# Two mixtures of experts around an attention: the second product of each block turned round, so that it gives rows at once

## Time and profile before

| | us |
|---|---|
| median of 3 runs | 1285.2 (1285.19 to 1287.82) |
| the profiled execution | 1283.73 |
| its span in the profile | 1282.0 |
| TensorE busy | 1144.8 (89%) |
| VectorE busy | 1124.8 (88%) |
| ScalarE busy | 878.0 (68%) |
| GpSimd busy | 518.6 (40%) |

### The profile page before, as it was taken

How to read it: one execution, slowest core, us unless ns; L and a number is a source line. 1 busy time by engine, 2 the same in 40 slices (tenths; PEclk the granted TensorE clock), 3 DMA queues, 4 the chain that set the end, 5 groups by cost and what they waited for, 6 DMA issues and landing times.

```text
span 1282.0 us, 27027 instructions
## 1 busy us (share of the span) xinstructions
PE 1144.8 (89%) x9003; PEld 606.4 (47%) x9003; DVE 1124.8 (88%) x2287; ACT 878.0 (68%) x1849; POOL 518.6 (40%) x672
## 2 busy tenths in 40 slices
PE   3857999888699999999999999999999999999993
PEld 2745888877322222332223223222222367788882
DVE  7877888887799999989999999999999778988885
ACT  1223555555289999898889888898887965455651
POOL 3883556424224001525336333445344128543232
PEclk9999999999689999999999999999999999999997
DMA  8115565563110200012011000010000413555653
GB/s 278 53 63 181 206 204 194 196 238 137 51 51 18 68 18 4 16 31 55 2 31 37 21 18 18 20 42 10 18 9 25 147 72 142 193 206 191 243 200 141
DMA packets 58746, 123.28 MB, mean 96 GB/s; under 512 B 12736, under 2 KB 33954, under 8 KB 58576
## 3 DMA queue, kind: packets, MB, share of 16 engines
q1 hardware_dynamic: 49616, 103.57, 23.6%
q0 software_dynamic: 8704, 16.93, 4.2%
q10 hardware_dynamic: 288, 1.05, 0.2%
HBM read 36.39 MB, written 23.62 MB: 47 GB/s over the span
## 4 chain that ended last, share of the span: by engine, by line
PE 59%; DVE 25%; POOL 6%; issue 5%; DMA 3%; ACT 2%; SPq 1%; DVEq 0%; POOLq 0%; ACTq 0%
PE psum L2329 15%; DVE att_neg_part L1996 13%; PE psum L2301 9%; PE psum L2232 8%; PE psum L2220 7%; PE psum L2222 7%; PE psum L2283 6%; POOL rows_dram L1293 4%; DVE ffn_x2c L1938 2%; DMA ffn_block_rows<-rows_dram 2%; DVE ffn_hidden L1949 2%; DVE stats L1631 1%; PE psum L2307 1%; ACT ffn_silu L1454 1%; PE psum L2172 1%
## 5 line engine op out<-in xcount | busy, mean ns | idle before, releaser
L1996 DVE TENSOR_REDUCE att_neg_part<-psum 128x2 f32<-128x1024 f32 x512 | 594.7, 1215 | 27.0 <-PE psum L2283 24.9
L1486 ACT ACTIVATE att_probs<-psum 128x512 f32<-128x512 f32 x1024 | 556.4, 597 | 59.8 <-PE psum L2301 23.0
L2329 PE MATMUL psum<-att_probs,att_values 128*18 128x256 f32 x4096 | 322.2, 387 | 4.3 <-issue 3.7
L2283 PE MATMUL psum<-att_right,att_left 62*128 62x512 f16 x1024 | 288.1, 391 | 31.0 <-DVE att_neg_part L1996 30.1
L1454 ACT ACTIVATE ffn_silu<-ffn_x2c,ffn_rec 128x256 f32<-128x256 f32 (+1 forms) x320 | 154.7, 487 | 170.4 <-DVE ffn_x2c L1938 169.9
L1309 POOL DMA_INDIRECT y_dram<-ffn_y,ffn_block_rows x144 | 142.6, 990 | 233.9 <-ACT ffn_y L1472 205.5
L2301 PE MATMUL psum<-att_right,att_left 64*128 64x512 f16 x512 | 199.0, 389 | 0.1
L2307 PE MATMUL psum<-att_right,att_left 64*128 64x512 f16 x512 | 194.9, 381 | 0.0
L1938 DVE TENSOR_SCALAR ffn_x2c<-psum,ffn_rec 128x256 f32<-128x256 f32 (+1 forms) x320 | 162.6, 512 | 34.0 <-PE psum L2222 29.7
L2220 PE MATMUL psum<-ffn_block_t,ffn_rec 128*128 128x256 f32 (+1 forms) x640 | 178.7, 361 | 1.8 <-ACT ffn_block_t L1405 1.8
L2222 PE MATMUL psum<-ffn_block_t,ffn_rec 128*128 128x256 f32 (+1 forms) x640 | 178.0, 360 | 0.0
(11 more groups left out here) (236 smaller groups left out, 1040.8 us busy)
## 6 DMA issues: line engine op xcount, KB each, us to landing
ffn_rec<-record SPq DMA_DIRECT2D x80, 776.5 KB, 3.8
ffn_block_rows<-rows_dram SPq DMA_DIRECT2D x64, 130.0 KB, 3.1
record<-in_L_ffn_W SPq DMA_DIRECT2D x16, 256.0 KB, 6.4
att_left<-q_parts_dram SPq DMA_DIRECT2D x64, 64.0 KB, 2.2
att_right<-att_max_parts SPq DMA_DIRECT2D x256, 1.0 KB
y_dram<-ffn_y,ffn_block_rows POOLq DMA_INDIRECT x144, 2.3
x_sb<-in_L_attn_x SPq DMA_DIRECT2D x4, 512.0 KB, 7.1
record<-in_L_ffn_Wo SPq DMA_DIRECT2D x8, 256.0 KB, 7.2
```

The costliest lines, as they stand in the source:

```text
L1486: S.activation(probs[:, slot % PROBS, :], ring_bank(("score", slot))[:, :], ACT.Exp, scale=unlift).then_inc(att_bank.by_act, 1)
L1996: V.tensor_reduce(out=neg_part[:, h % 2, keys, p::PAIR, t], in_=psum[:, low:high + 1, :], axis=AX.X, op=ALU.max, negate=True).then_inc(red ...
L2283: product = TE.matmul(bank[max_banks(n)[k]], left[s][PRODUCTS[k], p, q], right[s][PRODUCTS[k], p, seen], start=True, stop=True)
L2329: last = TE.matmul(value_bank[g * VS:g * VS + 2 * VW, p * HALF // 2:(p + 1) * HALF // 2], values_flat[:, at:at + 2 * VW], queries, start=( ...
```

## The change

- `tensor_second`: hidden is loaded and Wo is streamed, in pieces of 128 rows: 8 matmuls of 128 columns for a long block where there were 4 of 256. y comes out with its rows on the partitions. `y_bank` has that shape; `back_bank`, `tensor_turn_back`, the buffer `y_t` and the semaphore `y_turned_back` are gone.
- bo lies along the free axis now. It leaves the record; instead SP loads it as a broadcast row for every block (`bo_rows`, 128 x 128 numbers, one more DMA in `sync_load_record`), and VectorE adds it out of PSUM (`vector_add_y`, in the place of `vector_clip_y`). That add now waits for the scatter of three blocks ago, and frees the seat (`y_added` in place of `biased`).
- The clip of y goes to GpSimd (`pool_clip_y`), behind the scatters of the block before; `scalar_weigh` waits for it and works in place in SBUF. `scalar_bias` is gone.
- Attention's first matmul waits for `y_added` where it waited for `weighed`.

```diff
         def sync_next_block(k, i):
-            Q.wait_ge(biased, k * BLOCKS + i - SLOTS[k] + 1)
+            Q.wait_ge(y_added, k * BLOCKS + i - SLOTS[k] + 1)
             sync_load_record(k, i)
...
             Q.dma_start(mix[k].rec[:, seat(k, i), :].unsqueeze(1),
                         record[:, bass.ds(expert, 1), :]).then_inc(mix[k].rec_in[seat(k, i)], 16)
+            Q.dma_start(mix[k].bo_rows[:, seat(k, i), :],
+                        bo[bass.ds(expert, 1), :].to_broadcast([P, F])).then_inc(mix[k].rec_in[seat(k, i)], 16)
...
                 if at >= 2:
                     pool_scatter_results(k, at - 2)
+                if 1 <= at <= BLOCKS:
+                    pool_clip_y(k, at - 1)
+
+        def pool_clip_y(k, i):
+            n = k * BLOCKS + i
+            G.wait_ge(y_added, n + 1)
+            y = mix[k].y[:, n % YSETS, 0:tiles_of(n), :]
+            G.tensor_scalar(y, y, LIMIT, -LIMIT, ALU.min, ALU.max).then_inc(y_clipped, 1)
...
-        def scalar_bias(k, i):
...
         def scalar_weigh(k, i):
             n, s = k * BLOCKS + i, seat(k, i)
-            S.wait_ge(turned_back, n + 1)
-            if n >= YSETS:
-                S.wait_ge(scattered_y[n % YSETS], y_scatters(n, n % YSETS))
+            S.wait_ge(y_clipped, n + 1)
             for r in range(tiles_of(n)):
-                last = S.activation(mix[k].y[:, n % YSETS, r, :], back_bank[n % 2][:, r * P:(r + 1) * P], ACT.Copy,
+                last = S.activation(mix[k].y[:, n % YSETS, r, :], mix[k].y[:, n % YSETS, r, :], ACT.Copy,
                                     scale=mix[k].block_rows[:, i % ROW_SLOTS, r, GATE:GATE + 1])
...
-        def vector_clip_y(k, i):
...
+        def vector_add_y(k, i):
+            n, s = k * BLOCKS + i, seat(k, i)
+            tiles = tiles_of(n)
+            V.wait_ge(product, n + 1)
+            if n >= YSETS:
+                V.wait_ge(scattered_y[n % YSETS], y_scatters(n, n % YSETS))
+            V.tensor_tensor(mix[k].y[:, n % YSETS, 0:tiles, :], y_bank[n % 2][:, 0:tiles, :],
+                            mix[k].bo_rows[:, s, :].unsqueeze(1).to_broadcast([P, tiles, F]), ALU.add).then_inc(y_added, 1)
...
         def tensor_attention():
-            TE.wait_ge(weighed, BLOCKS)
+            TE.wait_ge(y_added, BLOCKS)
...
             TE.wait_ge(hidden_ready, n + 1)
             if n >= 2:
-                TE.wait_ge(biased, n - 1)
-            few = slice(0, rows_of(n))
-            for c in range(HC):
-                last = TE.matmul(y_bank[n % 2][:, few], mix[k].rec[:, s, WO + c * F:WO + (c + 1) * F], mix[k].hidden[:, n % 2, c, few],
-                                 start=(c == 0), stop=(c == HC - 1))
+                TE.wait_ge(y_added, n - 1)
+            for r in range(tiles_of(n)):
+                for c in range(HC):
+                    last = TE.matmul(y_bank[n % 2][:, r, :], mix[k].hidden[:, n % 2, c, r * P:(r + 1) * P],
+                                     mix[k].rec[:, s, WO + c * F:WO + (c + 1) * F], start=(c == 0), stop=(c == HC - 1))
             last.then_inc(product, 1)
```

More of the change, by code:

```diff
@@ L413, in build_macaron @@
         product = semaphore("second_product")
-        biased = semaphore("y_biased")
+        y_added = semaphore("y_added")
         y_clipped = semaphore("y_clipped")
-        turned_back = semaphore("y_turned_back")
         weighed = semaphore("y_weighed")
@@ L1594, in vector_fold @@
             V.wait_ge(fold_dve, 2)
-            V.tensor_copy(record[:, :, BO], bo_col)
             V.tensor_scalar(record[:, :, CLIP_LO:CLIP_LO + HC], bias[1], -1.0, -X2_LIMIT,
@@ L1894, in build_macaron @@
         chunk_bank = [bank[0], bank[1], bank[2], wide[0][:, 0:512]]
-        y_bank = [bank[3][:, 0:BLOCK], wide[1][:, 0:BLOCK]]
+        y_bank = [rows[:, 0:BH * F].rearrange("p (r f) -> p r f", r=BH) for rows in (bank[3], wide[1])]
         turn_bank = [bank[5][:, 0:BLOCK], bank[5][:, BLOCK:2 * BLOCK]]
-        back_bank = [bank[3][:, BLOCK:2 * BLOCK], wide[1][:, BLOCK:2 * BLOCK]]
         def vector_experts(k):
```

49 lines of the change are left out of this document (9 added, 40 removed).

## The result

The changed kernel takes 1298.8 us (median of 4 runs, 1296.8 to 1301.9) against 1285.8 (4 runs, 1285.2 to 1287.8): ratio 1.0098, 95% interval 1.0085 to 1.0110. It is slower, by 13 us in the medians; the two profiled executions, spans 1296.1 and 1282.0, differ by 14.1.

What follows compares the result with a forecast made beforehand. TensorE was taken to pace long blocks, VectorE close behind, rows' transfers the first mixture's short blocks. Terms -7.5 + 1.5 + 5 + 7.5 + 4 - 1.7 = +8.8 gave 1292.5, put on the median: 1294 us (1280 to 1306).

Steps and rivals of the forecast that it cites:

- the sum: All terms against the profiled execution's 1283.73 us: -7.5 + 1.5 + 5 + 7.5 + 4 - 1.7 = +8.8.
- One of its own signs of being wrong: Long blocks: the prediction counts as wrong if the pitch between chores isn't 5.45 us.
- TensorE's pace, -7.5: Long blocks: turns back save 0.22, second product 1.78 against 1.73; net -0.17 in 44 blocks, 7.5 us gained.
- the VectorE-bound blocks' +1.5: VectorE's add replacing its clip costs 0.1 in 15 blocks where VectorE is the bound: 1.5 us.
- The rule for which weight loads would not hide: Second product: loads overlap only across differing row groups, giving product near 3.4, block near 7.1; rival 1340, chance 0.01.
- GpSimd's queue in the first mixture, +5: Blocks 16 to 19 and 21: clip behind chores makes ScalarE's weighing 8.1 late; holes recover 3, cost 5 (2.5 to 10).
- the lower bound 0.35: GpSimd's clip of y: lowest price, from half a 512-column cast at 0.605; 1.1 taken, range 0.35 to 1.5.
- GpSimd's queue in the second mixture, +7.5: Block 2's clip waits behind chores and scatters, weighing 7.6 later; with later blocks 7.5 us (5 to 10).
- SP and the short blocks, +4: First mixture's short blocks: rows asked for 0.45 later plus new DMA's 0.50; 4 x 1.0 = 4 us (2.5 to 6).
- Into attention, -1.7: Last second product to attention's first matmul: 2.3 us becomes the add's 0.5, saving 1.7.
- the clip and VectorE fight over the port: SBUF port in every block: 0.5 to 0.9 each over 64 long blocks, up to 40 us, 1310 and more; chance 0.07.

Runs made afterwards that it cites:

- the second set: Second of three sets of four kernels: kernel before, changed kernel, bo transfer behind the rows, both costs away; the kernel before took 1285.1 us there.
- e4: Kernel before, with only the second product in 8 matmuls of 128 columns instead of 4 of 256, weights and moving operand unchanged; 1.0079 of the kernel before.
- r2: Changed kernel, unmodified, run again in the second set; 1.0115 of the kernel before.
- e7: Changed kernel with bo loaded only once into each seat and GpSimd's clip of y left out; 0.9975 of the kernel before.
- r3: Changed kernel without GpSimd's clip of y, repeated in the third set; 1.0081 of the kernel before.
- r4: Changed kernel with bo loaded only once into each seat, GpSimd's clip kept, repeated in the third set; 1.0000 of the kernel before.
- e5: Changed kernel with the bo transfer issued after the rows' transfer of the same block instead of ahead of it; 1.0067 of the kernel before.
- e8: Kernel before plus an unread transfer of a quarter of the expert's bo to 128 partitions behind each record; 1.0041 of the kernel before.
- e1: Changed kernel without GpSimd's clip of y, in the first set; 1.0084 of the kernel before.

## Why the prediction was right

It said 1294 us (1280 to 1306), slower with 0.63; it is 1298.8, so the loss is 13.0 where the sum had 8.8. The mechanism was right in the two parts that carry the loss, the queue in the second mixture and the short blocks; of the sizes, two were well off. One of its own signs of being wrong came about: the pitch is 5.54, not 5.45. By its terms, measured in the second set:

- **TensorE's pace, -7.5.** The turns back are gone as forecast, but the second product takes 1.86 or 1.89 mostly, not 1.78, so that the pitch is 5.54 and not 5.45: at most 44 x 0.08 = 3.5 us. With both costs away the long stretches (w0 to w22, and w5 to w39 of the second mixture) are 0.8 and 1.9 shorter, 2.7 together, in which the VectorE-bound blocks' +1.5 is contained: the two terms together were -6.0. The rule for which weight loads would not hide (the Trainium skill, page "TensorE: Matmul & The Clock Gate", section "The mechanism") would have given 3.4 for the product, by an estimate. The trace disagrees: 1.78 to 1.89 with the values of hidden as weights, mostly 1.78 in e4 with the record's. (The same section of the Trainium skill lets a load also run ahead into the background weight buffer, which the prediction passed over; no run here tells whether this is what happens.) The price of reversing the operands, 0.005 a pass, is no more than seen; its cause is open.
- **GpSimd's queue in the first mixture, +5.** This is the term of the sum that was most mis-sized. It is at most +0.3: r2 and e7 are 1.0 apart (123.10 against 122.09), but r3 and r4 give 0.7 of that to the `bo` transfers. ScalarE did wait for the clip there, 8.8 us in all over the first mixture (one wait of 3.8 among them has its like in e7, 3.3 for VectorE's add), where some 8 were forecast. But nearly all of it was swallowed before it reached TensorE; the prediction let VectorE's holes take back only 3. The clip took 0.44 (0.77 beside VectorE's clip of hidden), not 1.1, and the blocks of copy and memset came out 0.9 late, with a pitch of 5.85 for three of them. The estimate from the nearest row, 1.26 with columns of scalars, was too high by more than two times; the lower bound 0.35 was the better one.
- **GpSimd's queue in the second mixture, +7.5.** It is +7.1 (38.35 against 31.23; the other difference between these two kernels, the `bo` transfers, is taken to have no part in it, as argued above), ScalarE's wait 6.4 where 7.6 was forecast. Here the clip's own length hardly matters, since the wait is chores and scatters. That half of the step which said *where* was exact.
- **SP and the short blocks, +4.** It is +5.3 (+8.0 in the traces of the first measurement), at a place and by a transfer as forecast: 1.1 us later to the rows in the block shown, 0.6 of it a register load that the prediction hadn't priced, and behind one wait of 4 us another 2.7 by the lower clock, which it hadn't either. Shown by e5 (the place alone gives 6.0 back), and by e8 in part (the transfer alone slows the kernel before by 0.41%, 1.9 to 3.8 us of it in this stage).
- **Into attention, -1.7.** It is -1.5 (0.50 against 2.04).

That the sum came as near as it did is luck: two errors cancel, for the gain in the long blocks was overrated by 3 to 4 us and the cost of GpSimd in the first mixture by nearly 5. The case for slower was right for the reasons given, the size was not.

The rival "the clip and VectorE fight over the port" didn't come about: the clip of hidden is 0.733 on average (0.715 before). (Its price of "up to 40" doesn't follow from its own 0.5 to 0.9 over 64 blocks, which is 32 to 58.) Where the two do meet, it is as little as this (blocks 16 and 17, VectorE's clip of hidden 203.85 to 204.87):

```profile
204.35 0.77 POOL L1309 TENSOR_SCALAR ffn_y<-ffn_y 128x256 f32<-128x256 f32 x1
```

0.33 more than alone, and VectorE's own took 1.02 instead of the 0.69 that it takes alone; it is 0.99 to 1.02 at all four places where only this clip starts within it. The Trainium skill (page "SBUF — State Buffer", section "Who interferes with whom") has whichever comes first hold the ports to its end. By that VectorE's, which began first, would not have been longer, and this clip would have ended at 204.87 + 0.44 = 205.31; it ended at 205.12. So both gave way a little, as far as the profile's rough ends on GpSimd can be trusted; the sizes are too small to matter to the time.

## What to carry to other kernels

An operation that is off the critical path on its own engine can put that engine's whole queue on it: before an engine is given work that somebody waits for closely, look for its longest run of chores, not at its share of busy time. A transfer that is added to a queue costs by its place, here far more than by its bytes; issue first what is waited for first, and count the instruction behind it. And where a stall is removed and the time doesn't move, look whether another of the same size has taken its place, and repeat where that one is absent before concluding that the first was free. For that, have a trace of the kernel before in every set of runs; here two sets lack it, and their ratios can't be divided into causes.

## What was not expected of the hardware

- A register load on SyncE right behind a transfer that broadcasts one 512-byte row to 128 partitions takes 0.86 to 0.88 us in the median and up to 1.24; behind the record's transfer 0.26 to 0.28, and 0.27 too in e5, where SyncE waits for a semaphore in between. e8 has 0.86 in the median and up to 1.21 with rows of 128 bytes, so the bytes don't make it.
- A GpSimd tensor_scalar of 128x256 with two constants takes 0.44 us, with two columns of scalars 1.26.
- 16 float32 passes of 128 columns take 1.78 in 45 of 64 products with the record as weights (e4), and 1.86 or 1.89 in 50 of 64 with the values of hidden as weights.
- In two of the three sets ScalarE or VectorE stands for 2.7 to 8.5 us early in the second mixture with no releaser in the trace, in kernels with and without the change (e4 and e8 for the latter), unless GpSimd's clip has held them up just before. In e1 it stands for a signal of TensorE whose matmuls the trace has as long done. What it is stays open. In those sets the kernel before is 10 to 15 us slower than in the other.
